# Summing gathered rows feature-major: the gathered rows become the stationary operand, and the copy and transpose of each window's sums go

## The chip, the cores and the metric

The kernel runs on one core of a Trainium2 chip. The metric is the device time of one execution in microseconds (us). TensorE is called PE here (its weight loads are a row of their own, PEld), VectorE DVE, ScalarE ACT, GpSimd POOL, and SyncE SP.

## What is computed

Two graph networks in a row over 2,500 nodes of 256 features and 82,500 edges, sorted by the node that receives them. All is float32. The part that the change touches is the first network, which has two layers:

```
edge_index = stack([src, dst])
for l in range(2):                       # RelGraphConv with a basis
    W = einsum('rb,bio->rio', coeff[l], basis[l])      # 8 relations
    all_h = einsum('ni,rio->rno', h, W)
    msg = all_h[etype, src] * norm
    h = segment_sum(msg, dst, 2500) + bias[l]          # relu after the first
x = layernorm(x + h)
```

The second network (an input product, three layers of `relu(mean of neighbours @ W_agg + h @ W_self + b)`, an output product, a layer norm of x plus the result) runs after it, in the "mean layers" below.

## The kernel before

**Tiles and windows.** The edges are cut into T = 645 tiles of 128. For each tile POOL issues an indirect DMA (`rows_of`, L250) that gathers the 128 source rows (1 KB each) into one of NG = 16 slots of `G`. DVE builds a selector `S` of 128 x 128 (L455, one of NSL = 8 slots): the row of an edge holds its weight in column 16 * relation + (destination minus the window's first node). Three tiles (TA = 3) make a window, of which a layer has NA = 215. PE sums the three tiles of a window in a PSUM bank (L662): `S` is stationary, the gathered rows move, and the sum is node-major, 128 selector columns on the partitions and 256 features along the bank.

**Turning the sums.** The later product wants them with the features on the partitions. So ACT copies each window's sum to `Zs` (L560), PE transposes its two halves into bank 4 or 5 (`pe_turn`, L650), and DVE adds them at the window's place in `ZA` (`dve_add`, L444), where ten windows overlap. After ten windows (30 tiles, a large window) PE multiplies `ZA` by the relations' weights, sixteen products spread over eight tiles (`pe_apply`, L615), adds what is carried over (L620), and ACT copies the product out (L519).

**Beside it.** Between the tiles, the kernel counts the edges between each two nodes for the second network: DVE builds two one-hot tables per tile (L378, L379), PE multiplies them (L593) and carries a window's overlap on (L598), ACT casts the counts (L505, L508), SP stores them. DVE also mixes the weights of the relations.

**The order.** Each engine's program is unrolled, and tile t comes in the same place on all of them. Waits are on semaphores that only count up:

- POOL gathers tile n once tile n - 16 has been summed (`s_sum`).
- DVE builds the selector of tile t + 5 at step t, once tile t - 3 has been summed. At each step with t % 3 = 1 it then adds window (t - 4) // 3, after that window's transposes (`s_turn`).
- ACT copies a window after its third tile (`s_sum`), and reports with `s_zs`.
- PE waits for a tile's rows (`s_land`) and selector (`s_sel`). At each step with t % 3 = 1 it transposes the window that ended two tiles earlier. Written for window k: tile 3k+2 ends it, PE goes on with tiles 3k+3 and 3k+4, and then waits for the copy of window k (`s_zs`) before anything behind it can start. `pe_turn` also waits for the addition of window k - 2 (`s_za`).

Both layers go this way one after the other, 1,290 tiles in all. Then come the mean layers (`pe_mean_layers`), with no gathers, in which PE multiplies counts by node rows (L828). L319 loads a register with a window's place, L494 clears `ZA`.

Of the kernel before, what the change touches and what calls it, by code (L numbers as in the profile page):

```python
# [94 lines left out]
def program(nc, x, ramp, ramp_col, srcT, dstT, etT, wT, large, small, basis, coeff, bias, W_in, b_in, W_agg, W_self,  # L95
# [11 lines left out]
    with ExitStack() as ctx:  # L107
# [3 lines left out]
        def sem(name):  # L111
            return ctx.enter_context(nc.semaphore(name))
# [59 lines left out]

        with ExitStack() as inner:
            RY = inner.enter_context(nc.sbuf_tensor("RY", [128, 20480], F32))
        (Mr, Nr, Aw, Aw8, E2, G, S, Zs, W2, ZA, Ew, Pg, hw, h1w, xw, xT) = lay(
            RY, ((NSL, 128), BF16), ((NSL, NB), BF16), ((4, NB), BF16), ((4, NB), U8), ((2, 128), BF16), ((NG, 256), F32),
            ((NSL, 128), F32), ((2, 256), F32), ((2, 2048), F32), ((2, 16 * ZC), F32), ((2, 128), F32), ((2, 256), F32),
            ((2, 256), F32), ((2, 256), F32), ((2, 256), F32), ((2, 256), F32))
        ZA = ZA.rearrange("p s (q c) -> p s q c", c=ZC)
        diag = [v[:, k, h * 128:(h + 1) * 128] for v in (xw, xT) for k in range(2) for h in range(2)]  # L180
# [5 lines left out]
        x1b = sb("x1b", [128, 4, 256], F32)  # L186
        assert EARLY * 512 + NR * CH <= 8512

        bank = [ctx.enter_context(nc.psum_tensor(f"bank{i}", [128, 512], F32)) for i in range(8)]


        s_src, s_dst, s_et, s_wgt, s_base, s_bas0, s_bas1, s_wts = (
# [5 lines left out]
        s_land = [sem(f"s_land{i}") for i in range(NG)]  # L198
        s_sel, s_sum = sem("s_sel"), sem("s_sum")

        s_zs, s_turn, s_za = sem("s_zs"), sem("s_turn"), sem("s_za")

        s_clear, s_carry1, s_prod, s_pg = sem("s_clear"), sem("s_carry1"), sem("s_prod"), sem("s_pg")
        s_hw, s_h1w, s_h1 = sem("s_hw"), sem("s_h1w"), sem("s_h1")
# [228 lines left out]
        def dve_add(e, l, w):  # L433

            g, wi = divmod(w, SW)
            wg = l * NA + w
            r = row_base(e, off[0:1, w:w + 1], 127)
            o = ZA[:, g % 2, :, bass.ds(r, 16)]
            if wi == 0:
                e.wait_ge(s_clear, 4 * (l * NW + g + 1))  # L440
            else:
                e.wait_ge(s_za, wg)
            e.wait_ge(s_turn, wg + 1)
            e.tensor_tensor(o, o, bank[4 + wg % 2][:, 0:256].rearrange("p (q c) -> p q c", c=16), ALU.add).then_inc(s_za, 1)  # L444

        def dve_layer(e, l):
            for t in range(T + (TAIL if l == 0 else 2)):
# [97 lines left out]
        def act_layer(e, l):  # L545
            for t in range(T + (TAIL if l == 0 else 2)):
                n = l * T + t
                if t == 0:
                    if l == 0:
                        e.wait_ge(s_zero, 1)  # L550
                    for k in range(4):
                        act_clear(e, l, 0, k)
                if t % TW in (24, 25, 26, 27) and t // TW + 1 < NW and t < T:
                    act_clear(e, l, t // TW + 1, t % TW - 24)
                if t % TA == TA - 1 and t < T:
                    wg = l * NA + t // TA
                    if wg > 1:
                        e.wait_ge(s_turn, wg - 1)
                    e.wait_ge(s_sum, n + 1)
                    e.copy(Zs[:, wg % 2, :], bank[2 + wg % 2][:, 0:256]).then_inc(s_zs, 1)  # L560
                for g, k in STEPS[l].get(t, []):
                    act_post(e, l, g, k)
                if l == 0 and t < 8 * WPE:
                    act_weight(e, t)
                if t < T:
                    for a in COUNTS.get(n, []):
                        act_counts(e, a)
                    if n in A_LOADS:
                        j = A_LOADS.index(n)
                        if j == 0:  # L570
                            e.wait_ge(s_ad, 16 * NA)
                            e.wait_ge(s_chore, NCH)
                            e.wait_ge(s_w1p, 8 * WPE)
                            e.wait_ge(s_prod, NW)
                        e.dma_start(A_sb[0:PB, j, :], Ad[j * PB:(j + 1) * PB, 0:N]).then_inc(s_A, 16)
# [63 lines left out]
                                      xT[:, s, c * 128:(c + 1) * 128], start=(c == 0), stop=(c == 1))  # L639
                mm.then_inc(s_win, 1)  # L640

        def pe_turn(e, l, w):
            wg = l * NA + w
            if wg > 1:
                e.wait_ge(s_za, wg - 1)
            else:
                e.wait_ge(s_idn, 1)
            e.wait_ge(s_zs, wg + 1)
            for c in range(2):
                mm = e.transpose(bank[4 + wg % 2][:, c * 128:(c + 1) * 128], Zs[:, wg % 2, c * 128:(c + 1) * 128], idn[:, :])  # L650
            mm.then_inc(s_turn, 1)

        def pe_layer(e, l):
            for t in range(T + (TAIL if l == 0 else 2)):
                n = l * T + t
                if t < T:
                    i, wg, k = t % TA, l * NA + t // TA, edge_rows(t)
                    if i == 0 and wg > 1:
                        e.wait_ge(s_zs, wg - 1)
                    e.wait_ge(s_sel, n + 1)  # L660
                    e.wait_ge(s_land[n % NG], 16 * (n // NG + 1))
                    e.matmul(bank[2 + wg % 2][:, 0:256], S[0:k, n % NSL, :], G[0:k, n % NG, :], start=(i == 0),  # L662
                             stop=(i == TA - 1)).then_inc(s_sum, 1)
                for g, k in STEPS[l].get(t, []):
                    if k < 8:
                        pe_apply(e, l, g, k)
                    elif l == 1:
                        pe_post(e, g, k)
                if t >= 4 and t % TA == 1 and t - 2 < T:
                    pe_turn(e, l, (t - 4) // TA)  # L670
                if l == 0 and t < 8 * WPE:
                    pe_weight(e, t)
                if t < T:
                    for a in COUNTS.get(n, []):
                        pe_counts(e, a)
# [137 lines left out]
        def pe_aggregate(e, l, c, j):  # L813
            n, i = (l * NC + c) * JB + j, l * NC + c
            bs = (2 * (i % 2), 2 * (i % 2) + 1)
            if j == 0:
                if i == 0:
                    e.wait_ge(s_pg, 2 * NW)
                    e.wait_ge(s_put, 2 * (NW - 1))
                elif i == 1:  # L820
                    e.wait_ge(s_zs, 2 * NA)
                else:
                    e.wait_ge(s_mean, 2 * (i - 1))
            e.wait_ge(*converted(n))
            e.wait_ge(s_lo, l * JB + j + 1)
            for mo in range(2):
                for q in range(2):
                    mm = e.matmul(bank[bs[mo]][:, 0:CH], hs[0:PB, j, q, mo * 128:(mo + 1) * 128], Ar[0:PB, n % NR, :],  # L828
                                  start=(j == 0 and q == 0), stop=(j == JB - 1 and q == 1))
            mm.then_inc(s_agg, 1)  # L830
# [43 lines left out]
        def sp_load_x1(e, j):  # L874
            if j == 0:
                e.wait_ge(s_x1d, 16 * NW)
                e.wait_ge(s_x1t, NW)
            if j >= 4:
                e.wait_ge(s_y, j - 3)
            e.dma_start(x1b[0:PB, j % 4, :], X1[j * PB:(j + 1) * PB, :]).then_inc(s_x1b[j % 4], 16)  # L880
# [81 lines left out]

        def act_mean_layers(e):
            last = NW - 1
            e.wait_ge(s_turn, 2 * NA)
            e.wait_ge(s_ad, 16 * NA)
            e.wait_ge(s_A, 16 * JB)
            for n in range(NR):
# [26 lines left out]

        def dve_mean_layers(e):
            last = NW - 1
            e.wait_ge(s_turn, 2 * NA)
            e.wait_ge(s_ad, 16 * NA)
            dve_carry1(e, 1, last)  # L1000
            for j in range(4):
# [404 lines left out]
```

## Time and profile before

| | |
|---|---|
| runs shown | 2393.61, 2394.03, 2397.88 us |
| median | 2394.03 us |
| the profiled execution's own time | 2401.69 us |
| its span, first to last instruction | 2399.9 us |
| mean granted PE clock in it | 0.889 of full speed |
| busy: PE, PEld, DVE, ACT, POOL | 75%, 56%, 50%, 26%, 52% of the span |

The busy share of PE counts recorded matmuls, whose ends the profiler models. The idle time of an engine stands behind the group of instructions that it precedes, with what ended it; "issue" is time for which the profile shows no wait, "remote" a release that it could not put down to an instruction. The gathers run to about 1,975 us, and the rest is the mean layers.

### The profile page before, as it was taken

Reading aid. Unit: us, or ns where it says so; the run is one execution under the profiler, and the core shown is the slowest. Engines: PE = TensorE matmul, PEld = TensorE weight load, DVE = VectorE, ACT = ScalarE, POOL = GpSimd, SP = SyncE. Lnnn points to the kernel's source line nnn. Section 1 sums busy time; section 2 is a strip of 40 time slices with the busy share of each in tenths; the row PEclk is TensorE's granted clock in tenths of the full one; section 3 lists DMA queues with packets and bytes.
Section 4 is the critical chain, followed back from the end, with each engine's and each line's share of the span. In section 5 each row is a group of like instructions: output and inputs, shape, how many; then the busy total and the mean of one; then the engine's idle time right before and its main releaser. Section 6 shows DMA issues by size and latency. Waiting matters only on the chain.

```text
span 2399.9 us, 29813 instructions
## 1 busy us (share of the span) xinstructions
PE 1803.5 (75%) x7695; PEld 1342.2 (56%) x7695; DVE 1197.4 (50%) x3965; ACT 625.7 (26%) x1520; POOL 1255.5 (52%) x1294
## 2 busy tenths in 40 slices
PE   4667677677677676757677777776666679999997
PEld 2455455455455454535455555555555567777776
DVE  5747654544445445335555555553268743232355
ACT  1112222222222222212222322222111124633332
POOL 5766666666666666366666666666666630000000
PEclk9879888988889899879989888899888789999998
DMA  6333333333333333233333333334533320000011
GB/s 209 93 89 97 99 98 98 100 97 98 99 99 97 99 99 99 59 92 101 102 100 98 105 99 100 103 101 122 169 102 96 98 61 11 1 1 1 1 35 44
DMA packets 118622, 208.19 MB, mean 87 GB/s; under 512 B 53828, under 2 KB 74196, under 8 KB 118456
## 3 DMA queue, kind: packets, MB, share of 16 engines
q0 software_dynamic: 62016, 169.04, 24.8%
q1 hardware_dynamic: 48848, 26.08, 3.8%
q10 hardware_dynamic: 7592, 11.13, 1.4%
q8 instruction: 71, 1.16, 0.2%
q14 instruction: 95, 0.78, 0.1%
HBM read 189.01 MB, written 17.13 MB: 86 GB/s over the span
## 4 chain that ended last, share of the span: by engine, by line
PE 50%; another core or an unknown queue 17%; issue 14%; DVE 13%; ACT 3%; DVEq 2%; DMA 1%; ACTq 0%; POOL 0%
PE bank L662 15%; PE bank L828 11%; PE bank L615 8%; DVE RY L455 4%; PE bank L650 4%; DVE RY L444 2%; PE bank L593 2%; PE bank L845 2%; PE bank L773 2%; DVE RY L379 1%; DVE RY L378 1%; DMA RX<-in_basis 1%; ACT RY L560 1%; DVE rdeg L390 1%
## 5 line engine op out<-in xcount | busy, mean ns | idle before, releaser
L662 PE MATMUL bank<-RY 128*128 128x256 f32 x2580 | 864.3, 432 | 11.6 <-issue 4.6
L250 POOL DMA_INDIRECT RY<-H,si x645 | 619.4, 960 | 367.0 <-issue 152.4
L250 POOL DMA_INDIRECT RY<-in_x,si x645 | 635.8, 986 | 333.1 <-issue 147.5
L444 DVE TENSOR_TENSOR RY<-RY,bank 128x256 f32 x430 | 180.8, 420 | 900.7 <-remote 694.8
L662 PEld LDWEIGHTS bank<-RY 128*128 128x128 f32 x2580 | 487.1, 220 | 109.4 <-issue 42.0
L650 PE MATMUL bank<-idn,RY 128*128 128x128 f32 x860 | 193.4, 311 | 394.7 <-issue 245.9
L455 DVE TENSOR_SCALAR RY<-iot,c,wgt 128x128 f32<-128x128 f32 x1290 | 461.8, 370 | 1.5 <-issue 1.5
L560 ACT COPY RY<-bank 128x256 f32<-128x256 f32 x430 | 161.1, 375 | 973.2 <-PE bank L662 519.8
L650 PEld LDWEIGHTS bank<-idn,RY 128*128 128x128 f32 x860 | 116.5, 158 | 503.4 <-issue 451.0
L828 PE MATMUL bank<-Ar,hs 125*128 125x500 f32 x1200 | 305.8, 405 | 0.0
L828 PEld LDWEIGHTS bank<-Ar,hs 125*128 125x128 f32 x1200 | 225.7, 188 | 51.7 <-issue 9.2
L593 PE MATMUL bank<-RY 128*128 128x320 bf16 x645 | 214.1, 333 | 16.2 <-DVE RY L379 8.4
L615 PE MATMUL bank<-RX,RY 128*128 128x256 f32 x704 | 202.8, 417 | 29.3 <-issue 25.3
L615 PE MATMUL bank<-RY 128*128 128x256 f32 x704 | 198.7, 410 | 18.6 <-DVE RY L444 12.7
L379 DVE TENSOR_SCALAR RY<-iotN,bcol 128x320 bf16<-128x320 f16 x645 | 196.0, 304 | 0.0
L615 PEld LDWEIGHTS bank<-RX,RY 128*128 128x128 f32 x704 | 146.8, 211 | 59.7 <-issue 31.5
L378 DVE TENSOR_SCALAR RY<-iotN,c 128x128 bf16<-128x128 f16 x645 | 178.9, 277 | 0.0
L615 PEld LDWEIGHTS bank<-RY 128*128 128x128 f32 x704 | 143.8, 206 | 47.3 <-DVE RY L444 16.1
L505 ACT CAST RY<-bank 128x320 bf16<-128x320 f32 x215 | 92.2, 429 | 249.3 <-remote 190.5
L740 ACT CAST Ar<-RX 125x500 fp32r<-125x500 uint8 x200 | 119.2, 609 | 99.2 <-PE bank L828 99.1
L494 ACT COPY RY<-zero 128x576 f32<-128x576 f32 x176 | 113.3, 680 | 0.0
L593 PEld LDWEIGHTS bank<-RY 128*128 128x128 bf16 x645 | 68.8, 107 | 69.0 <-issue 32.5
(106 smaller groups left out, 1163.2 us busy)
## 6 DMA issues: line engine op xcount, KB each, us to landing
RY<-in_x,si POOLq DMA_INDIRECT x645
RY<-H,si POOLq DMA_INDIRECT x645
Ad<-RY SPq DMA_DIRECT2D x215, 40.0 KB
RX<-Ad ACTq DMA_DIRECT2D x20, 305.2 KB
RX<-in_basis ACTq DMA_DIRECT2D x2, 2048.0 KB, 34.3
H<-RY SPq DMA_DIRECT2D x22, 128.0 KB
RY<-in_x SPq DMA_DIRECT2D x22, 128.0 KB
X<-RY SPq DMA_DIRECT2D x22, 128.0 KB
```

Source lines behind the costliest of these rows:

```text
L250: e.indirect_dma_start(G[0:k, n % NG, :], None, table, bass.IndirectOffsetOnAxis(ap=si[0:k, t:t + 1], axis=0)).then_inc(s_land[n % NG], 16)
L378: e.tensor_scalar(Mr[:, u % NSL, :], iotN[:, 0:128], c1[:, u:u + 1], None, ALU.is_equal)
L379: e.tensor_scalar(Nr[:, u % NSL, :], iotN[:, :], bcol[:, u:u + 1], None, ALU.is_equal).then_inc(s_hot, 1)
L444: e.tensor_tensor(o, o, bank[4 + wg % 2][:, 0:256].rearrange("p (q c) -> p q c", c=16), ALU.add).then_inc(s_za, 1)
L455: e.tensor_scalar(S[:, v % NSL, :], iot[:, :], c2[:, u:u + 1], wgt[:, u:u + 1], ALU.is_equal, ALU.mult).then_inc(s_sel, 1)
L560: e.copy(Zs[:, wg % 2, :], bank[2 + wg % 2][:, 0:256]).then_inc(s_zs, 1)
L593: e.matmul(b[:, 0:NB], Mr[0:k, a % NSL, :], Nr[0:k, a % NSL, :], start=(i == 0), stop=(w == 0 and i == TA - 1)).then_inc(s_cnt, 1)
L615: mm = e.matmul(bank[0][:, 0:256], ZA[:, s, q, 0:128], W[:, c, r * 256:(r + 1) * 256], start=(q == 0), stop=(g == 0 and q == 15))
L650: mm = e.transpose(bank[4 + wg % 2][:, c * 128:(c + 1) * 128], Zs[:, wg % 2, c * 128:(c + 1) * 128], idn[:, :])
L662: e.matmul(bank[2 + wg % 2][:, 0:256], S[0:k, n % NSL, :], G[0:k, n % NG, :], start=(i == 0), stop=(i == TA - 1)).then_inc(s_sum, 1)
L740: e.copy(o, i_).then_inc(s_arA, 1)
L828: mm = e.matmul(bank[bs[mo]][:, 0:CH], hs[0:PB, j, q, mo * 128:(mo + 1) * 128], Ar[0:PB, n % NR, :], start=(j == 0 and q == 0), stop=(j == ...
```

## The change

PE sums the tiles the other way round: half of the gathered rows (128 features) is stationary, and the selector moves. A tile takes two matmuls of 128 columns, one for each half of the features, in place of one of 256. The sum stands feature-major in PSUM at once. The two halves go to two banks (2 and 4, or 3 and 5 for the other window of a pair), which are now declared as one tensor of two banks (`pair`), so that DVE adds both with one instruction, straight from the sums. The ACT copy, `Zs`, the transposes, and the semaphores `s_zs` and `s_turn` go. DVE's addition stays at its step and now waits for `s_sum`. The first tile of window k waits for the addition of window k - 2.

```diff
-        (Mr, Nr, Aw, Aw8, E2, G, S, Zs, W2, ZA, Ew, Pg, hw, h1w, xw, xT) = lay(
+        (Mr, Nr, Aw, Aw8, E2, G, S, W2, ZA, Ew, Pg, hw, h1w, xw, xT) = lay(
...
-        bank = [ctx.enter_context(nc.psum_tensor(f"bank{i}", [128, 512], F32)) for i in range(8)]
+        pair = [ctx.enter_context(nc.psum_tensor(f"pair{i}", [128, 2, 512], F32)) for i in range(2)]
+        bank = [None if i in (2, 3, 4, 5) else ctx.enter_context(nc.psum_tensor(f"bank{i}", [128, 512], F32)) for i in range(8)]
+        for i in range(4):
+            bank[2 + i] = pair[i % 2][:, i // 2, :]
...
# dve_add
-            o = ZA[:, g % 2, :, bass.ds(r, 16)]
+            o = ZA[:, g % 2, :, bass.ds(r, 16)].rearrange("p (a b) c -> p a b c", a=2)
...
-            e.wait_ge(s_turn, wg + 1)
-            e.tensor_tensor(o, o, bank[4 + wg % 2][:, 0:256].rearrange("p (q c) -> p q c", c=16), ALU.add).then_inc(s_za, 1)
+            e.wait_ge(s_sum, l * T + min(T, TA * w + TA))
+            e.tensor_tensor(o, o, pair[wg % 2][:, :, 0:128].rearrange("p a (b c) -> p a b c", c=16), ALU.add).then_inc(s_za, 1)
...
# act_layer
-                if t % TA == TA - 1 and t < T:
-                    wg = l * NA + t // TA
-                    if wg > 1:
-                        e.wait_ge(s_turn, wg - 1)
-                    e.wait_ge(s_sum, n + 1)
-                    e.copy(Zs[:, wg % 2, :], bank[2 + wg % 2][:, 0:256]).then_inc(s_zs, 1)
...
-        def pe_turn(e, l, w):
-            wg = l * NA + w
-            if wg > 1:
+        def pe_sums_of(e, l, t):
+
+            n, i, wg, k = l * T + t, t % TA, l * NA + t // TA, edge_rows(t)
+            if i == 0 and wg > 1:
                 e.wait_ge(s_za, wg - 1)
-            else:
-                e.wait_ge(s_idn, 1)
-            e.wait_ge(s_zs, wg + 1)
+            e.wait_ge(s_sel, n + 1)
+            e.wait_ge(s_land[n % NG], 16 * (n // NG + 1))
             for c in range(2):
-                mm = e.transpose(bank[4 + wg % 2][:, c * 128:(c + 1) * 128], Zs[:, wg % 2, c * 128:(c + 1) * 128], idn[:, :])
-            mm.then_inc(s_turn, 1)
+                mm = e.matmul(bank[2 + 2 * c + wg % 2][:, 0:128], G[0:k, n % NG, c * 128:(c + 1) * 128], S[0:k, n % NSL, :],
+                              start=(i == 0), stop=(i == TA - 1))
+            mm.then_inc(s_sum, 1)
...
# pe_layer
-                    i, wg, k = t % TA, l * NA + t // TA, edge_rows(t)
-                    if i == 0 and wg > 1:
-                        e.wait_ge(s_zs, wg - 1)
-                    e.wait_ge(s_sel, n + 1)
-                    e.wait_ge(s_land[n % NG], 16 * (n // NG + 1))
-                    e.matmul(bank[2 + wg % 2][:, 0:256], S[0:k, n % NSL, :], G[0:k, n % NG, :], start=(i == 0),
-                             stop=(i == TA - 1)).then_inc(s_sum, 1)
+                    pe_sums_of(e, l, t)
...
-                if t >= 4 and t % TA == 1 and t - 2 < T:
-                    pe_turn(e, l, (t - 4) // TA)
```

At the ends of the layers, the waits for `s_zs`, `s_turn` and `s_x1t` become waits for `s_za`, `s_sum` and `s_win`.

The order on PE before, from tile 180 of the first layer, which begins window 60 (L662 sums a tile, L650 is a transpose, L593 and L598 are the counts, L615 a product of `ZA`):

```order
L662 MATMUL bank2<-RY 128x256 [waits s_land4,s_sel,s_zs]
L593 MATMUL bank6<-RY 128x320 [waits s_hot,s_aw8]
L662 MATMUL bank2<-RY 128x256 [waits s_land5,s_sel]
L650 MATMUL bank5<-idn,RY 128x128 [waits s_zs,s_za]
L650 MATMUL bank5<-idn,RY 128x128
L662 MATMUL bank2<-RY 128x256 [waits s_land6,s_sel]
L593 MATMUL bank6<-RY 128x320 [waits s_hot]
L662 MATMUL bank3<-RY 128x256 [waits s_land7,s_sel,s_zs]
```

The same stretch of the changed kernel (L648 sums half a tile, L591 is a count):

```order
L648 MATMUL pair0<-RY 128x128 [waits s_land4,s_sel,s_za]
L648 MATMUL pair0<-RY 128x128
L591 MATMUL bank6<-RY 128x320 [waits s_hot,s_aw8]
L648 MATMUL pair0<-RY 128x128 [waits s_land5,s_sel]
L648 MATMUL pair0<-RY 128x128
L648 MATMUL pair0<-RY 128x128 [waits s_land6,s_sel]
L648 MATMUL pair0<-RY 128x128
L591 MATMUL bank6<-RY 128x320 [waits s_hot]
L648 MATMUL pair1<-RY 128x128 [waits s_land7,s_sel,s_za]
```

Between the second and the third tile stood two transposes of the window before, with a wait for its copy. Now nothing stands there, and a window's first tile waits for an addition in place of a copy.

On DVE before, at step 181, which adds window 59:

```order
L455 TENSOR_SCALAR RY<-iot,c2,wgt 128x128 [waits s_sum]
L319 TENSOR_LOAD off
L319 ISA x2
L444 ISA [waits s_turn,s_za]
L444 TENSOR_TENSOR RY<-RY,bank5 128x16x16
L455 TENSOR_SCALAR RY<-iot,c2,wgt 128x128 [waits s_sum]
```

And of the changed kernel:

```order
L459 TENSOR_SCALAR RY<-iot,c2,wgt 128x128 [waits s_sum]
L323 TENSOR_LOAD off
L323 ISA x2
L448 ISA [waits s_sum,s_za]
L448 TENSOR_TENSOR RY<-RY,pair1 128x16x16
L459 TENSOR_SCALAR RY<-iot,c2,wgt 128x128 [waits s_sum]
```

The addition stands where it stood; only what it waits for is another semaphore.

## Rows read from the trace of the kernel before

**Rows 1.** The page: span, busy time by engine, and POOL in 40 slices.

```profile
span 2399.9 us, 29813 instructions
...
PE 1803.5 (75%) x7695; PEld 1342.2 (56%) x7695; DVE 1197.4 (50%) x3965; ACT 625.7 (26%) x1520; POOL 1255.5 (52%) x1294
...
POOL 5766666666666666366666666666666630000000
```

**Rows 2.** Stretches of 100 us: busy us (instructions) by engine, PEclk, DMA share, GB/s.

```profile
100.00:200.00 100.00, 64.01 (x253) 47.09 (x251) 51.69 (x155) 16.31 (x41) 67.52 (x69) 0.78 0.33 95
500.00:600.00 100.00, 75.01 (x329) 54.35 (x328) 48.71 (x203) 25.46 (x67) 65.57 (x68) 0.87 0.35 99
1700.00:1800.00 100.00, 70.37 (x288) 56.15 (x287) 52.32 (x111) 15.68 (x40) 64.56 (x69) 0.83 0.43 127
```

**Rows 3.** The page's costliest groups: busy, mean ns, idle before them and releaser.

```profile
L662 PE MATMUL bank<-RY 128*128 128x256 f32 x2580 | 864.3, 432 | 11.6 <-issue 4.6
L250 POOL DMA_INDIRECT RY<-H,si x645 | 619.4, 960 | 367.0 <-issue 152.4
L250 POOL DMA_INDIRECT RY<-in_x,si x645 | 635.8, 986 | 333.1 <-issue 147.5
L444 DVE TENSOR_TENSOR RY<-RY,bank 128x256 f32 x430 | 180.8, 420 | 900.7 <-remote 694.8
L662 PEld LDWEIGHTS bank<-RY 128*128 128x128 f32 x2580 | 487.1, 220 | 109.4 <-issue 42.0
L650 PE MATMUL bank<-idn,RY 128*128 128x128 f32 x860 | 193.4, 311 | 394.7 <-issue 245.9
L560 ACT COPY RY<-bank 128x256 f32<-128x256 f32 x430 | 161.1, 375 | 973.2 <-PE bank L662 519.8
```

**Rows 4.** POOL's waits: us in total, times, longest.

```profile
POOL RY L250 <- PE bank L662: 210.9, 222, 9.8
POOL RY L250 <- remote: 151.8, 107, 2.5
POOL RY L250 <- DMA H<-RY: 33.0, 1, 33.0
```

**Rows 5.** Timeline from 621.9 us: start, duration, instruction, idle before it.

```profile
621.90 0.38 PE L650 MATMUL bank<-idn,RY 128*128 128x128 f32 x2
...
622.11 0.60 PE L662 MATMUL bank<-RY 128*128 128x256 f32 x2
...
622.55 0.30 PE L593 MATMUL bank<-RY 128*128 128x320 bf16 x1
...
624.25 0.59 PE L662 MATMUL bank<-RY 128*128 128x256 f32 x2
625.20 0.94 POOL L250 DMA_INDIRECT RY<-in_x,si  x1 [0.30 <-issue]
626.06 0.37 ACT L560 COPY RY<-bank 128x256 f32<-128x256 f32 x1 [4.43 <-PE bank L662]
...
626.45 0.95 POOL L250 DMA_INDIRECT RY<-in_x,si  x1 [0.30 <-issue]
...
626.58 0.41 PE L650 MATMUL bank<-idn,RY 128*128 128x128 f32 x2 [1.73 <-issue]
```

**Rows 6.** Timeline of PE from 650 us.

```profile
650.71 0.60 PE L662 MATMUL bank<-RY 128*128 128x256 f32 x2
...
651.85 0.59 PE L662 MATMUL bank<-RY 128*128 128x256 f32 x2
659.09 0.66 PE L650 MATMUL bank<-idn,RY 128*128 128x128 f32 x2 [6.65 <-issue]
```

**Rows 7.** Timeline of ACT from 650 us.

```profile
658.57 0.37 ACT L560 COPY RY<-bank 128x256 f32<-128x256 f32 x1 [2.21 <-remote]
```

**Rows 8.** Timeline of PE from 1,230 us: eight float32 passes of 128 columns.

```profile
1236.25 1.05 PE L638 MATMUL bank<-RY,wts 128*128 128x128 f32 x8
1237.14 0.30 PE L593 MATMUL bank<-RY 128*128 128x320 bf16 x1
```

More of the change, by code:

```diff
@@ L174, in program @@
             RY = inner.enter_context(nc.sbuf_tensor("RY", [128, 20480], F32))
-        (Mr, Nr, Aw, Aw8, E2, G, S, Zs, W2, ZA, Ew, Pg, hw, h1w, xw, xT) = lay(
+        (Mr, Nr, Aw, Aw8, E2, G, S, W2, ZA, Ew, Pg, hw, h1w, xw, xT) = lay(
             RY, ((NSL, 128), BF16), ((NSL, NB), BF16), ((4, NB), BF16), ((4, NB), U8), ((2, 128), BF16), ((NG, 256), F32),
-            ((NSL, 128), F32), ((2, 256), F32), ((2, 2048), F32), ((2, 16 * ZC), F32), ((2, 128), F32), ((2, 256), F32),
+            ((NSL, 128), F32), ((2, 2048), F32), ((2, 16 * ZC), F32), ((2, 128), F32), ((2, 256), F32),
             ((2, 256), F32), ((2, 256), F32), ((2, 256), F32), ((2, 256), F32))
@@ L199, in program @@
         s_sel, s_sum = sem("s_sel"), sem("s_sum")
-        s_zs, s_turn, s_za = sem("s_zs"), sem("s_turn"), sem("s_za")
+        s_za = sem("s_za")
         s_clear, s_carry1, s_prod, s_pg = sem("s_clear"), sem("s_carry1"), sem("s_prod"), sem("s_pg")
@@ L820, in pe_aggregate @@
                 elif i == 1:
-                    e.wait_ge(s_zs, 2 * NA)
+                    e.wait_ge(s_za, 2 * NA)
                 else:
@@ L876, in sp_load_x1 @@
                 e.wait_ge(s_x1d, 16 * NW)
-                e.wait_ge(s_x1t, NW)
+                e.wait_ge(s_win, NW)
             if j >= 4:
@@ L964, in act_mean_layers @@
             last = NW - 1
-            e.wait_ge(s_turn, 2 * NA)
+            e.wait_ge(s_sum, 2 * T)
             e.wait_ge(s_ad, 16 * NA)
@@ L997, in dve_mean_layers @@
             last = NW - 1
-            e.wait_ge(s_turn, 2 * NA)
+            e.wait_ge(s_sum, 2 * T)
             e.wait_ge(s_ad, 16 * NA)
```

## The prediction

> **What bounds the kernel now.** I read the page first [rows 1]. No engine is busy all the time: PE 75% of the span and POOL 52%, and POOL's slices are at 6 tenths, evenly, until the gathers end at about 1,975 us. The mean layers behind them have no gathers and no window sums, so the change can only act before. There are 430 windows of three tiles.
>
> The stretches [rows 2] say how this part keeps time. POOL issues 68 or 69 gathers in 100 us, that is 1.45 to 1.47 us for a tile and 4.35 to 4.41 us for a window. It does so with the counts (500 to 600 us, PE busy 75.0) and without them (100 to 200 and 1,700 to 1,800 us, PE busy 64.0 and 70.4). Work comes and goes on PE and the pace stays: the amount of PE's work is not the bound.
>
> POOL itself could go faster. Two gathers that nothing holds up start 1.25 us apart [rows 5], 0.95 us of work and 0.30 us of its own issue. Its idle time is 367.0 + 333.1 = 700.1 us [rows 3]. Of this 1290 x 0.30 = 387 us is its own issue, and 33.0 us the wait for the first layer's rows [rows 4]. The other 280 us is waiting for a slot, that is for PE to report tile n - 16 as summed ("PE bank L662" and "remote").
>
> Why is PE late, if it has time? The timeline [rows 5] shows it. PE transposes at 621.90 us, sums the next tile at 622.11 us and two more by 624.85 us, and stands still for 1.73 us until the next transposes at 626.58 us. These wait for ACT's copy, which starts at 626.06 us, although the matmuls of the window's last tile end at 622.71 us by the record and ACT has been idle for 4.43 us. So the report of that sum reached ACT about 3.35 us late. Thirty microseconds on it is worse: sum over at 651.31 us [rows 6], copy at 658.57 us [rows 7], 7.26 us later, and PE idle for 6.65 us. I don't know what delays these reports. That they are late is what sets the pace: transposes of window k - 1, last sum of window k, report, copy, transposes of window k. Each window makes this round trip by itself. It costs 0.21 (transposes) + 0.44 (sum) + 0.37 (copy) + the delay, and some 0.15 us of signalling, so 1.2 us + the delay. The mean of 4.4 us leaves 3.2 us for the delay and for PE's other work before the transposes. The idle time ahead of the copies, 973.2 us, and ahead of the transposes, 394.7 us [rows 3], is this trip seen from two engines.
>
> **The change, part by part.**
>
> *Sums.* 1290 tiles change from two recorded passes of 256 columns to four of 128 (a float32 matmul has two). Before, a tile takes 622.55 - 622.11 = 0.44 us [rows 5]. Eight float32 passes of 128 columns with weights of their own, back to back, take 1237.14 - 1236.25 = 0.89 us [rows 8], 0.111 us each, so four take 0.44 us. A window stays at 1.33 us. The weight load's own row has a mean of 220 ns [rows 3]. If it were not hidden, a tile would take 0.88 us; that is the upper bound, and 0.44 us the lower one. I take 0.44 us, because rows 8 are the same shape and type. The Trainium skill, "Perfetto Trace Analysis", Matmuls, says that larger matmuls are more efficient than smaller ones when possible. By it PE's work would grow; it gives no figure, and between these two rows the trace does not bear it out.
>
> *Transposes.* 430 pairs of 0.21 us go from PE, 90 us. They lie beside waiting, and are worth nothing by length alone. With them goes the wait in which PE stood.
>
> *Copies.* 430 copies of 375 ns go from ACT (161 us busy [rows 3]). ACT bounds nothing at 26%, so only their place in the trip counts.
>
> *Addition.* DVE's instruction has as many elements, from two banks. The nearest row is the present one, 420 ns; two instructions' worth, 840 ns, is the upper bound. DVE has 900.7 us of idle time ahead of it [rows 3], which hides 181 us more. I take no change. It stands at the same step of DVE's order. Behind it are the selectors, but those of five tiles ahead are made by then; it now waits for a sum instead of a transpose made two tiles later, so it comes free earlier.
>
> *New wait.* The first tile of window k waits for the addition of window k - 2, hence for the report of tile 3k - 4, and three tiles lie between. At POOL's own pace four tiles take 5.0 us. Of these 0.44 us is the sum, 0.42 us the addition and some 0.1 us signalling, so that delays up to 4.0 us cost nothing. Before, at that pace, the limit was 3.75 - 1.2 = 2.6 us. More than this margin counts that two windows are in the trip together: a batch of late reports lets six tiles through, where it now lets through three, and the 16 slots then absorb what is left.
>
> *The ends of the layers* save one copy and one pair of transposes each, about 1 us. I leave it out.
>
> *The sum.* With no wait for slots, POOL would bound: 2401.7 (the profiled execution) - 280 = 2122 us. One of the two delays that I looked at (7.26 us) is far beyond 4.0 us, so some stops of PE stay, and the slots do not cover all of them. I take two thirds of the 280 us as gone, 187 us: 2215 us. The ends that I keep are all of it and a third. The median of the runs shown is 7.7 us below the profiled execution, which gives **2207 us**.
>
> **The rivals.**
>
> *R1, POOL bounds.* The delays stay as they are, the slots cover them, and all 280 us go: 2122 - 7.7 = **2114 us**. For it: PE has idle time in every stretch [rows 2]. Against it: delays of 7 us.
>
> *R2, the reports come later still.* POOL's pauses go, and if the reports are delayed by the traffic of the gathers, each stop comes back at the addition's wait. A third of the 280 us is gained: 2401.7 - 93 - 7.7 = **2301 us**. For it: PE lay idle for 6.65 us while a report was still out [rows 6, 7], so the delay is not PE's own queue. Against it: I can't see a link to the gathers in these rows.
>
> *R3, slower.* The place is PE's completion of the sums. If the gap between recorded end and report is real work of PE that the record hides, PE has no spare time, and more passes cost their time in full. A window's sums and transposes are now 6 + 2 passes (2580 and 860 over 430 windows [rows 3]), and become 12. Four more at 0.111 us [rows 8] are 191 us, which gives 2394 + 191 = **2585 us**; at the weight load's 0.22 us they would be 378 us, 2772 us. It decides once PE's true time for a window is above 4.4 us. For it: nothing else in the rows explains the late reports. Against it: the pace is the same with and without the counts' passes [rows 2], and 6.65 us of idle PE is longer than any work queued before it. The Trainium skill, "Perfetto Trace Analysis", Tensor Engine Instruction, says that the profiler only estimates when a matmul ends. By that the gap may be hidden work, and R3 would be the case; the rows bear it out only in that the reports are late.
>
> *R4, no change.* What holds POOL is not this trip, or the addition's wait takes its place one for one: **2394 us**.
>
> **How the numbers follow.** A measurement of this kernel can tell about 0.2%, 5 us, from no change. Forecast (2130 to 2290 us) 0.50, R1 0.13, R2 (2290 to 2389 us) 0.17, R4 0.07, R3 0.13. So faster 0.80, same 0.07, slower 0.13. The range goes from just below R1, 2105 us, to R4, 2390 us. Beyond it lie R3, most of R4 and a little of R1, about 0.2. The forecast alone would have 2130 to 2290 us.
>
> **What would show it.** Right: more than 72 gathers in 100 us (the forecast has 1290 x 1.25 + 93 us of waiting, 1.32 us each, so 75 or 76); POOL's waits for L648 under 150 us; no ACT row for a copy; four passes of a tile in about 0.44 us; gathers over by about 1,790 us; the mean layers as long as before, some 425 us. R1: 80 gathers in 100 us. R2: PE idle ahead of the first tile of a window, released by DVE's addition, often for 3 us and more. R3: PE's idle time gone and under 68 gathers in 100 us, or passes of L648 0.2 us apart at the full clock. My argument fails if the pace stays while the copies are gone.

## The result, and the profile after

The change makes no gain: 2401.97 us median (2396.86 to 2405.13, 20 runs) against 2397.06 us (2392.14 to 2399.77, 20 runs) for the kernel before, beside it on the same chip. The ratio is 1.0023, 95% interval 1.0016 to 1.0029. I had predicted 2,207 us.

The page of the profiled execution after: span, busy time by engine, POOL in 40 slices.

```profile
span 2400.1 us, 31965 instructions
...
PE 1782.9 (74%) x9415; PEld 1484.7 (62%) x9415; DVE 1219.4 (51%) x3965; ACT 481.8 (20%) x1090; POOL 1246.4 (52%) x1294
...
POOL 5766666666666666466666666666666640000000
```

Against [rows 1] ACT has lost its 430 copies (1520 instructions became 1090), PE has 1,720 records more (2,580 more passes for sums, 860 fewer for transposes), and POOL looks the same in every slice.

The same stretches as in [rows 2]: busy us (instructions) of PE, PEld, DVE, ACT and POOL, PEclk, DMA share, GB/s.

```profile
100.00:200.00 100.00, 59.05 (x321) 51.14 (x321) 51.84 (x151) 7.87 (x19) 66.45 (x68) 0.78 0.33 93
500.00:600.00 100.00, 71.02 (x403) 59.09 (x402) 49.60 (x197) 17.89 (x44) 63.80 (x68) 0.87 0.35 98
1700.00:1800.00 100.00, 69.13 (x397) 61.58 (x395) 53.28 (x109) 7.99 (x18) 64.81 (x69) 0.84 0.43 129
```

Still 68 or 69 gathers in 100 us. Where did the waits go? The costliest groups (busy, mean ns, idle before them and releaser), to be read against [rows 3]:

```profile
L648 PE MATMUL pair<-RY 128*128 128x128 f32 x5160 | 907.9, 320 | 487.0 <-issue 251.5
L648 PEld LDWEIGHTS pair<-RY 128*128 128x128 f32 x5160 | 819.8, 228 | 625.5 <-issue 320.1
L254 POOL DMA_INDIRECT RY<-in_x,si x645 | 631.8, 980 | 341.6 <-issue 152.9
L254 POOL DMA_INDIRECT RY<-H,si x645 | 614.3, 952 | 370.8 <-issue 148.0
L459 DVE TENSOR_SCALAR RY<-iot,c,wgt 128x128 f32<-128x128 f32 x1290 | 450.3, 356 | 562.4 <-PE pair L648 374.0
L448 DVE TENSOR_TENSOR RY<-RY,pair 128x256 f32 x430 | 180.5, 420 | 314.3 <-remote 166.9
```

The addition is the same size (420 ns). PE had 394.7 us of idle time ahead of its transposes and 11.6 us ahead of its sums; now 487.0 us stand ahead of the sums. The list of waits (us in total, times, longest) says what for, as far as the profile shows a release:

```profile
PEld pair L648 <- issue: 320.1, 222, 6.5
POOL RY L254 <- issue: 300.8, 981, 1.1
PEld pair L648 <- DVE RY L448: 259.7, 129, 10.8
PE pair L648 <- issue: 251.5, 159, 6.1
POOL RY L254 <- PE pair L648: 223.9, 201, 5.7
PE pair L648 <- DVE RY L448: 217.7, 110, 10.2
...
POOL RY L254 <- remote: 157.2, 106, 3.3
```

PE now waits for DVE's addition, up to 10.2 us (and 251.5 us more with no release on record), and POOL waits 223.9 + 157.2 = 381 us for slots, where it waited 363 us [rows 4]. The timeline shows one stop (start, duration, instruction, idle before it):

```profile
620.15 0.61 PE L648 MATMUL pair<-RY 128*128 128x128 f32 x4
...
620.60 0.30 PE L591 MATMUL bank<-RY 128*128 128x320 bf16 x1
...
622.04 0.61 PE L648 MATMUL pair<-RY 128*128 128x128 f32 x4
...
622.73 0.30 PE L591 MATMUL bank<-RY 128*128 128x320 bf16 x1
623.47 0.35 DVE L459 TENSOR_SCALAR RY<-iot,c,wgt 128x128 f32<-128x128 f32 x1 [3.38 <-PE pair L648]
623.63 0.43 ACT L509 CAST RY<-bank 128x320 bf16<-128x320 f32 x1 [9.45 <-remote]
623.71 0.94 POOL L254 DMA_INDIRECT RY<-in_x,si  x1 [1.91 <-PE pair L648]
...
624.29 0.42 DVE L448 TENSOR_TENSOR RY<-RY,pair 128x256 f32 x1 [0.47 <-issue]
...
624.77 0.83 PE L648 MATMUL pair<-RY 128*128 128x128 f32 x4 [1.74 <-DVE RY L448]
```

DVE, ACT and POOL all start within 0.24 us of each other, after 3.38, 9.45 and 1.91 us of idling. The trace has a mark for a semaphore's update: three marks of the sums' reports and two of the counts' stand between 623.45 and 623.70 us. So a handful of PE's reports arrived together, and everyone who waited for one of them woke.

I followed this through the trace, from the recorded end of each sum to the next mark of its semaphore. Some marks are missing (there are 1,184 for 1,290 sums), so single delays are rough. Once the gathers are over, PE's marks come 0.01 us after the ends. In the gather part the median in each 100 us is 1.0 to 1.9 us from 100 to 1,700 us, and a tenth come over 3.4 us late. Only PE's are late: of DVE's reports on its selectors more marks are missing (753 stand for 1,290), but nine tenths of those in the gather part stand 0.01 us after an end, where by the same measure PE's stand 1.1 us after one in the median.

### The profile page after: what moved, and what is told of

It reads as the page before. It is cut to its first block, busy times and chain, and to the rows that moved or that the text cites. A ratio compares the mean times of both kernels' runs of the same rounds, so it can differ in the third digit from the quotient of the medians.

```text
span 2400.1 us, 31965 instructions
## 1 busy us (share of the span) xinstructions
PE 1782.9 (74%) x9415; PEld 1484.7 (62%) x9415; DVE 1219.4 (51%) x3965; ACT 481.8 (20%) x1090; POOL 1246.4 (52%) x1294
## 4 chain that ended last, share of the span: by engine, by line
PE 63%; issue 13%; another core or an unknown queue 11%; DVE 9%; DMA 1%; DVEq 1%; ACT 1%; ACTq 0%; POOL 0%; SPq 0%; POOLq 0%
PE pair L648 28%; PE bank L613 12%; PE bank L819 6%; PE pair L819 5%; PE bank L591 3%; DVE RY L459 3%; DVE RY L448 2%; PE pair L836 2%; PE bank L764 2%; PE bank L636 1%; DMA RX<-in_basis 1%; PE bank L596 1%; DVEq L323 1%; DVE RX L359 1%
## 5 line engine op out<-in xcount | busy, mean ns | idle before, releaser
L648 PE MATMUL pair<-RY 128*128 128x128 f32 x5160 | 907.9, 320 | 487.0 <-issue 251.5
L648 PEld LDWEIGHTS pair<-RY 128*128 128x128 f32 x5160 | 819.8, 228 | 625.5 <-issue 320.1
L254 POOL DMA_INDIRECT RY<-in_x,si x645 | 631.8, 980 | 341.6 <-issue 152.9
L254 POOL DMA_INDIRECT RY<-H,si x645 | 614.3, 952 | 370.8 <-issue 148.0
L448 DVE TENSOR_TENSOR RY<-RY,pair 128x256 f32 x430 | 180.5, 420 | 314.3 <-remote 166.9
L591 PE MATMUL bank<-RY 128*128 128x320 bf16 x645 | 216.5, 336 | 7.7 <-issue 3.9
L613 PE MATMUL bank<-RY 128*128 128x256 f32 x704 | 201.3, 413 | 7.3 <-DVE RY L448 5.6
L819 PE MATMUL bank<-Ar,hs 125*128 125x500 f32 x640 | 166.0, 406 | 0.0
L613 PEld LDWEIGHTS bank<-RY 128*128 128x128 f32 x704 | 133.8, 210 | 21.8 <-DVE RY L448 5.8
L819 PE MATMUL pair<-Ar,hs 125*128 125x500 f32 x560 | 142.1, 403 | 0.0
L819 PEld LDWEIGHTS bank<-Ar,hs 125*128 125x128 f32 x640 | 120.3, 188 | 27.6 <-issue 5.0
L819 PEld LDWEIGHTS pair<-Ar,hs 125*128 125x128 f32 x560 | 105.4, 188 | 24.1 <-issue 4.1
L523 ACT COPY RY<-bank 128x256 f32<-128x256 f32 x44 | 16.4, 372 | 431.3 <-remote 340.4
```

Source lines behind the costliest of these rows:

```text
L254: e.indirect_dma_start(G[0:k, n % NG, :], None, table, bass.IndirectOffsetOnAxis(ap=si[0:k, t:t + 1], axis=0)).then_inc(s_land[n % NG], 16)
L448: e.tensor_tensor(o, o, pair[wg % 2][:, :, 0:128].rearrange("p a (b c) -> p a b c", c=16), ALU.add).then_inc(s_za, 1)
L591: e.matmul(b[:, 0:NB], Mr[0:k, a % NSL, :], Nr[0:k, a % NSL, :], start=(i == 0), stop=(w == 0 and i == TA - 1)).then_inc(s_cnt, 1)
L613: mm = e.matmul(bank[0][:, 0:256], ZA[:, s, q, 0:128], W[:, c, r * 256:(r + 1) * 256], start=(q == 0), stop=(g == 0 and q == 15))
L648: mm = e.matmul(bank[2 + 2 * c + wg % 2][:, 0:128], G[0:k, n % NG, c * 128:(c + 1) * 128], S[0:k, n % NSL, :], start=(i == 0), stop=(i == ...
```

## The experiments

The runs fell on several chips, and these are of two kinds. Each time is to be read beside the kernel before on the same chip. On two of the five chips the kernel before took 2,107 and 2,109 us (**prompt** chips below), on three, and on the one of the result, 2,371 to 2,398 us (**late** chips). Where no number of executions is given, it is one.

### Four cuts through the whole

Half the bytes of each gather (the sums take this half of the features twice; the cuts of code below show the lines that matter):

```diff
-G[0:k, n % NG, :], None, table, ...            # 1 KB for a row
+G[0:k, n % NG, 0:128], None, half, ...         # table as (2N, 128), 512 B
```

> The change with half the bytes of every gather: 128 columns of a row in place of 256 (the sums use this half twice, so the output is another one). Theory T (the traffic of the gathers holds back PE's reports): with half the bytes a report comes in half the delay, the pace rises from 68 to over 73 gathers in 100 us, below 2,250 us. Theory P (PE's own time for its work, hidden by the record, sets the pace): no change, 2,390 to 2,410 us. Theory D (POOL's issue, not bytes): no change either.

One pass in place of two for each sum, `G` and `S` read as the upper halves of their float32:

```diff
+            G16 = G[0:k, n % NG, :].bitcast(BF16).rearrange("p (c h) -> p c h", h=2)[:, :, 1]   # S16 alike
...
```

> The change with the sums taken from the upper 16 bits of the rows and selectors, as bfloat16: two passes in a tile in place of four (the sums lose accuracy). Theory P: PE's time for a window falls by 6 of its 12 passes, so the pace rises at once to what POOL can do, under 2,200 us. Theory T: PE's work is beside the point, within 1% of 2,400 us. Theory D: the same as T.

Every sum twice:

```diff
-            for c in range(2):
+            for j in range(4):
+                c = j % 2
...
```

> The change with every sum taken twice (eight passes for a tile, 0.89 us in place of 0.44; the sums are twice as large). Theory P: 12 more passes in a window at 0.11 us or more, so at least 430 x 1.33 = 572 us longer, 2,970 us or more. Theory T and D: PE has room in a window of 4.4 us, 2,400 to 2,500 us, and the longer time only in the stretches where PE was nearly full.

No gathers after the first sixteen:

```diff
-            for n in range(FIRST, 2 * T):
+            for n in ():
...
# pe_sums_of
-            e.wait_ge(s_land[n % NG], 16 * (n // NG + 1))
+            e.wait_ge(s_land[n % NG], 16)
```

> The change without the gathers after the first 16 (PE sums these 16 tiles again and again; POOL is idle and H1 is not read). All other work and waits stay. Theory P: the pace stays, 2,350 to 2,400 us. Theory T: reports come at once, and the gather part (1,930 us) shrinks to what PE and DVE need, under 1,500 us, in all under 1,950 us. Theory D gives the same time as T, but T alone says that sums are reported in under 0.3 us here.

Measured: half bytes 2093.34, one pass 2105.85, twice 2118.27, no gathers 1632.94 us, and the kernel before 2107.22 us. This was a prompt chip, which none of the expectations had foreseen, so these times don't decide between their theories. With PE's work halved or doubled the time stays within 0.6% of the kernel before, and without the gathers it falls by 474 us: on this chip POOL's 1.25 us a gather is the bound. Twice the sums, stretch 500 to 600 us (columns as above):

```profile
500.00:600.00 100.00, 100.00 (x790) 94.65 (x790) 59.31 (x230) 20.00 (x49) 75.92 (x80) 1.00 0.41 115
```

PE is busy all the time and POOL still issues 80 gathers. In all four traces no 100 us of the gather part has a median or a 90th percentile of the report's delay above 0.01 us, and in the three that gather the gathers are faster than in the result. So gathers do not make reports late on every chip.

### The change and the kernel before again, POOL set free, fewer slots

> The change itself, word for word, timed against the kernel before on a chip on which the kernel before took 2,107 us in place of 2,397. On such a chip PE's reports were never late (0.01 us in four kernels). Theory T2 (late reports are a condition of the chip and set the pace only where they occur; elsewhere POOL's 1.25 us does): the change takes 2,100 to 2,115 us, within 0.5% of before, 79 gathers in 100 us. Theory L (the change is slower by its own work on DVE or PE): the difference of 5 us of the other chip stays or grows. On a chip of the slow kind: 2,402 against 2,397 us again.

> The kernel before, word for word, for its trace. T2: where it takes 2,107 us, its copies L560 start within 0.3 us of the end of the sum, POOL's waits for PE are under 60 us, and PE's stops ahead of the transposes are short. If its trace shows late reports at 2,107 us too, T2 falls.

POOL free: the gathers go round 15 slots that nobody reads, PE sums the rows in slot 0 again and again, and a tile's sum still waits for its gather's landing.

```diff
-                if n >= NG:
-                    e.wait_ge(s_sum, n - NG + 1)
+                e.wait_ge(s_land[slot(n)], 16 * (n_before(n)))   # landed before
...
```

> The change with POOL set free: PE sums slot 0 for every tile, the gathers go round the other 15 slots and wait for nothing but their slot's last landing; a tile's sum still waits until its gather has landed (the sums are of other rows). Theory T2, chip with prompt reports: POOL was waiting for little, 0 to 20 us gained, 1.25 to 1.27 us for each gather. Chip with late reports: gathers at 1.25 us, and the sums stay behind them by more than 16 tiles if the traffic holds the reports back (over 2,450 us), or follow them (2,120 us) if the 16 slots were the trouble.

Twelve slots:

```diff
-NG = 16
+NG = 12
...
-FIRST = 16
+FIRST = 12
```

> The change with 12 slots for gathered tiles in place of 16. Theory T2, chip with prompt reports: PE is seldom 12 tiles behind, 2,105 to 2,130 us. Chip with late reports: the pauses of POOL come earlier but the pace is set by the reports, within 1% of 2,402 us; if instead the slots' slack decides, over 2,450 us.

This was a late chip. The change took 2405.21 us (7 executions) against 2397.92 (10; ratio 1.0031, 1.0016 to 1.0046), the kernel before once more 2397.47, twelve slots 2400.01, and POOL set free **3290.91 us**. Its page shows PE and POOL in 40 slices of 82 us, and the granted clock between them:

```profile
PE   2100011101189999930001111011899987899998
...
POOL 7777777777500000067777777776000000000000
PEclk8555555555599999965555555555899998999999
```

While POOL gathers, PE does almost nothing; when POOL has finished a layer, PE catches up at full speed. By stretches:

```profile
100.00:200.00 100.00, 15.86 (x36) 8.63 (x35) 7.50 (x16) 1.17 (x3) 75.94 (x80) 0.52 0.36 104
500.00:600.00 100.00, 17.11 (x42) 11.71 (x43) 7.26 (x14) 0.00 (x0) 76.21 (x73) 0.52 0.33 95
...
1100.00:1200.00 100.00, 100.00 (x739) 91.74 (x738) 86.38 (x364) 32.10 (x78) 0.00 (x0) 1.00 0.07 18
```

And a piece of the timeline inside the first layer:

```profile
322.71 2.93 PE L655 MATMUL pair<-RY 128*128 128x128 f32 x12 [30.67 <-issue]
...
333.25 0.34 DVE L464 TENSOR_SCALAR RY<-iot,c,wgt 128x128 f32<-128x128 f32 x1 [9.02 <-remote]
...
344.45 0.34 DVE L464 TENSOR_SCALAR RY<-iot,c,wgt 128x128 f32<-128x128 f32 x1 [10.06 <-remote]
...
355.84 0.42 DVE L453 TENSOR_TENSOR RY<-RY,pair 128x256 f32 x1 [11.04 <-issue]
```

PE sums three tiles by 325.64 us. DVE, idle, gets one report 7.6 us later, the next 11.2 us after that, and the third, which lets it add, another 11 us later. The rows themselves landed as always: by the DMA packets, the last of a gather ended 2.4 us after its issue in the median, here, in the change and on the prompt chip. In the two stretches in which PE catches up there are no gathers, and the reports come 0.01 us after the sums' ends. So on this late chip it is the gather stream that holds back PE's reports, not PE's queue and not rows that come late. That goes with the second outcome named before the run (over 2,450 us). In the change POOL's wait for slots keeps it from coming to this: it stops POOL, and reports get through. The kernel without gathers never ran on a late chip.

### Is it the depth of the buffers, the bytes, or PE's work?

Four windows in flight: the six matmuls of a window are issued together at its third tile, so both halves fit one bank, and there are 14 selectors.

```diff
# pe_sums_of
-            if i == 0 and wg > 1:
-                e.wait_ge(s_za, wg - 1)
+            if t % TA < TA - 1:
+                return
+            if wg >= 4:
+                e.wait_ge(s_za, wg - 3)
...
```

> The change with more room for PE to run ahead of its own reports: the six matmuls of a window are issued together at its third tile, so that a window needs one PSUM bank and four windows are in flight in place of two, and 14 selectors in place of 8. Theory T2, chip with late reports: POOL's pauses are what lets the reports through, and each pause now frees up to 12 tiles in place of 6, so half of the 280 us of pauses goes, 2,250 to 2,300 us. Theory B (the balance between gathers and PE is in time, not in tiles: PE needs its share of the time without gathers however deep the buffers are): within 1% of 2,402 us. On a chip with prompt reports: 2,100 to 2,115 us.

The 14 selectors alone, made up to eleven tiles ahead:

```diff
-AHEAD = 6
+NSS = 14        # slots of S
+AHEAD = 12
...
```

> The change with 14 selectors in place of 8, nothing else. T2, late reports: two windows in flight still limit PE to six tiles, so no more than 1% from 2,402 us. B: the same. If it alone gains over 3%, it was DVE's selectors that made PE stop, and not the addition. Prompt reports: 2,100 to 2,115 us.

Two of the first four again, for a late chip:

> Half the bytes of every gather (128 columns of a row in place of 256, the sums use this half twice) once more, for a chip with late reports. If the bytes hold the reports back: over 73 gathers in 100 us, under 2,250 us. If it is the number of rows or POOL's own work on a gather: within 2% of 2,402 us. Prompt reports: 2,093 us again.

> Every sum taken twice once more (eight passes for a tile), for a chip with late reports. Theory T2 and B with reports as the scarce thing: PE has room, under 2,450 us. Theory B with PE's working time as the scarce thing: each microsecond of passes needs its own stretch without gathers, 1290 x 0.44 = 568 us more, 2,900 us or above. Prompt reports: 2,118 us again.

A late chip, the kernel before at 2371.18 us. Four windows 2378.66, selectors 2376.51, half bytes 2371.22, sums twice 2423.90 us. My theory that a stop frees as many tiles as PE may run ahead is wrong: with room for twelve POOL still gets 68 to 70 gathers in 100 us. Half the bytes bring nothing, so the amount of data is not the load. Doubling the sums, where PE needs 91 us of 100, costs about 2%:

```profile
500.00:600.00 100.00, 90.59 (x672) 82.28 (x671) 50.23 (x196) 17.14 (x42) 62.79 (x67) 0.98 0.35 98
```

### Data or descriptors, even spacing or full stops, number of reports

Gathers of 64 bytes for a row from the 17th tile on:

```diff
+            c = 256 if n < NG else 16
+            part = table if n < NG else table.rearrange("n (a b) -> (n a) b", b=16)
...
```

> The change with 64 bytes gathered for a row in place of 1,024 (from the 17th tile on; the sums are of other numbers), with as many rows, descriptors and instructions. If the data hold PE's reports back, they come at once now and the gathers run at 1.25 us: under 2,150 us. If descriptors or POOL's work do it: within 1.5% of the change, 67 to 69 gathers in 100 us. On a chip with prompt reports 2,090 to 2,110 us and nothing is told apart.

A memset of 128 columns on POOL after each gather, for which the next gather waits:

```diff
                 rows_of(e, n, x if n < T else H1)
...
+                e.memset(pause, 0.0).then_inc(s_pause, 1)
```

> The change with a short memset on POOL between two gathers, so that they start further apart (1.35 to 1.6 us) and evenly. Theory S (the pace is a time share: PE needs some 0.2 us without gather work for each tile, whenever it comes): if the spacing is up to 1.5 us, the pauses for slots shrink by as much and the time stays within 1.5% of the change. Theory F (reports come only when the gathers have stopped altogether): the pauses stay and the spacing adds to them, at least 1290 x 0.1 = 130 us more. Prompt reports: 1290 x spacing + 490 us.

The four windows again, with one report for each (the cut is against the four windows):

```diff
-                    if c == 1:
-                        mm.then_inc(s_sum, 1)
+            mm.then_inc(s_sum, 1)
...
```

> The change with four windows, 14 selectors and one report of PE for a window in place of three. If the number of PE's reports is what the path can't carry: 3% or more faster than the kernel before on this chip. If not: within 1% of it, as the same kernel with three reports was (2,379 against 2,371 us).

> The change without the gathers after the first 16, once more, for a chip with late reports. If the gathers alone hold the reports back: 1,633 us as on the chip with prompt reports (within 1.5%), and no late report. If the chip has slow reports by itself: over 1,700 us.

These fell on a prompt chip, the kernel before at 2108.86 us: tiny rows 2101.10, spaced 2220.12, one report 2104.19, no gathers 1628.65 us. They tell little of the late chips. Even 64 bytes for a row leave POOL at its 1.25 us, so that time does not depend on the bytes. The memset stretched the 1.25 us to 1.34 us and cost 111 us against the kernel before, close to 1274 x 0.09 = 115.

The last two:

> The change itself, timed again. On a chip with prompt reports (before at 2,107 to 2,109 us): POOL's 1.25 us for a gather is the bound of both kernels, so the change takes 2,104 to 2,112 us, within 0.3% of before. If the copies and transposes did cost something there, it is 0.5% faster or more. On a chip with late reports: 0.2 to 0.3% slower than before again.

> The change with a short memset on POOL after each gather, which stretched the 1.25 us between gathers to 1.34 us on the chip with prompt reports (2,220 us). On a chip with late reports: theory S (time share: what POOL leaves idle counts, whenever it does) has the pauses shrink by what the memsets take, within 1.5% of the change; theory F (reports pass only when the gathers have stopped altogether) has the pauses stay, 2,400 + 116 = 2,516 us or so. Prompt reports: 2,220 us again.

A late chip. The change took 2378.93 us (10 executions) against 2374.70 (13; ratio 1.0017, 1.0004 to 1.0029); with the memsets it took 2381.24 us. What cost 111 us on the prompt chip costs 2.3 us here. POOL's waits in the change on this chip:

```profile
POOL RY L254 <- PE pair L648: 177.8, 184, 5.6
POOL RY L254 <- remote: 167.6, 119, 4.0
```

and with the memsets:

```profile
POOL RY L254 <- PE pair L651: 102.9, 122, 5.8
POOL RY L254 <- remote: 77.0, 80, 2.4
```

345 us of waiting for slots became 180 us, and within the layers the gathers still start 1.48 us apart in the mean, as without the memsets. The expectation for a time share holds, the one for full stops (2,516 us) does not.

### What follows

| kernel | time, us | before on the same chip | kind | POOL's wait for slots, us |
|---|---|---|---|---|
| the change | 2405.2, 2378.9 | 2397.9, 2374.7 | late | 381, 345 |
| the kernel before | 2397.5 | 2397.9 | late | 369 |
| 12 slots | 2400.0 | 2397.9 | late | 386 |
| 4 windows with 14 selectors | 2378.7 | 2371.2 | late | 342 |
| 14 selectors alone | 2376.5 | 2371.2 | late | 342 |
| half bytes | 2371.2 | 2371.2 | late | 341 |
| sums twice | 2423.9 | 2371.2 | late | 430 |
| spaced | 2381.2 | 2374.7 | late | 180 |
| POOL free | 3290.9 | 2397.9 | late | none |
| half, tiny bytes | 2093.3, 2101.1 | 2107.2, 2108.9 | prompt | 157, 84 |
| one pass; twice | 2105.9; 2118.3 | 2107.2 | prompt | 80; 127 |
| one report | 2104.2 | 2108.9 | prompt | 35 |
| spaced | 2220.1 | 2108.9 | prompt | 40 |
| no gathers | 1632.9, 1628.7 | 2107.2, 2108.9 | prompt | |

(The last column adds POOL's waits for PE and "remote". Each has 0.3 us of POOL's own issue in it; half bytes on the prompt chip has 491 of them in its 157 us, so that hardly any waiting is left there.) On a late chip gathers and PE's reports share something. With POOL free the gathers come 1.25 to 1.42 us apart, by stretches of 100 us, and in the first layer PE sums 55 tiles between 100 us and the last gather at 881 us, one in 14 us; at 1.48 us in the mean, stops included, PE keeps up. The slots find that point by themselves, whatever the trip around them looks like, and for that reason neither buffers nor spacing nor the removed copies and transposes move it. That the gathers hold back the reports is shown by POOL set free. That a balance in time sets the pace is borne out by the spacing and the deeper buffers, one execution each; what lies between 1.42 and 1.48 us was not tried. What is shared is not known: not the data (half bytes), not PE's passes (5,160 more of them cost 9 ns each: 2423.9 - 2371.2 = 52.7 us over the kernel before, less the 4.2 us by which the change was slower on another late chip, is 48.5 us). Descriptors and the number of reports were to be told apart by tiny rows and one report, but both ran on a prompt chip only, and this stays open.

## Why the prediction was wrong, point by point

**What bounds the kernel.** Right: the amount of PE's work doesn't, and POOL could go at 1.25 us. The sum without any wait for slots, 2122 - 8 = 2114 us, is within 0.4% of what prompt chips show for the kernel before (2107.22, 2108.86). Wrong: the step "that they are late is what sets the pace", by the round trip transposes, sum, report, copy. The lateness was taken as given, a fixed delay that the trip adds up. On a late chip it is an answer to the gathers. I wrote that I don't know what delays the reports and went on to forecast what happens if the delay stays the same; it doesn't stay the same when POOL speeds up.

**Sums.** Right. Four passes take 0.45 us (620.15 to 620.60 us in the timeline), where 0.44 us was forecast. The Trainium skill, "Perfetto Trace Analysis", Matmuls, prefers larger matmuls; in this row the step from 256 to 128 columns costs 0.01 us a tile. **Addition** 420 ns, right. **Copies and transposes**: gone, worth nothing, as their length alone was said to be.

**New wait.** Its margin, delays up to 4.0 us, fitted the delays before, of which by the marks 8% are longer. But PE stops at it for 218 us in all, up to 10.2 us. In the stop that the timeline shows, the burst that lets DVE add is the same that lets POOL go on; that most stops are of this kind was not counted.

**The sum.** The failed step is "I take two thirds of the 280 us as gone", which rests on "That they are late is what sets the pace". None went. The sum that gave 280 us gives 299.5 us for the change: 341.6 + 370.8 us idle, less 387 us of issue and 25.9 us for the first layer's rows. In the list of waits 363 us became 381. In place of the trip, the runs show gathers and reports in balance: three ways around the slots (two windows in flight, four windows, 12 slots) give the same pace, and POOL without its stops leaves PE one tile in 14 us.

**The rivals.** R4, "what holds POOL is not this trip", 2,394 us, was the case and had 0.07. R2 had the mechanism, "if the reports are delayed by the traffic of the gathers, each stop comes back at the addition's wait", but let a third of the 280 us be gained; nothing was. Its sign was there before: PE idle for 6.65 us while a report was out [rows 6], and, in the trace of before, PE's marks 0.01 us after the ends wherever there were no gathers. R1's 2114 us is the prompt chip's time, though not by this change. R3 is refuted: 5,160 added passes cost some 48 us on a late chip and 11 us on a prompt one, not 0.111 us each. The Trainium skill, "Perfetto Trace Analysis", Tensor Engine Instruction, says that a matmul's end is estimated; the delay of 7.6 us after three tiles on an otherwise idle PE is no hidden work of that kind, because in the same trace the same passes are reported in 0.01 us once a layer's gathers are over.

**What would show it.** The signs did their work: gathers in 100 us (over 72 for right, found 68), POOL's waits for L648 (under 150 us, found 224), the last gather (by 1,790 us, found 1,958), all with the copies gone, as my sentence on what makes the argument fail has it. Of R2's sign, PE stopped by the addition often for 3 us and more, there are 110 stops of 2.0 us in the mean.

**The small loss.** The three measurements on late chips agree, 0.2 to 0.3%, 4 to 7 us. At the 9 ns above, 1,720 more passes would be 16 us, an estimate; what the copies and transposes that are gone give back was not measured, so the cause of the loss is not shown. What the change does on a prompt chip was not timed as it stands. Its neighbours there (one pass, one report) are 1.4 and 4.7 us below the kernel before, one run each.

## What to carry to other kernels

If a report is late while its engine idles, ask first where in the program it is late and where it isn't, and what else runs there. The trace of before answers it, and that would have been a reason to move chance from the forecast to R2 and R4. A ring of slots that seems to be too slow may be the regulator of something shared; a kernel that sets it free can show this in one run (here 3,291 us). And time a kernel beside its reference on more than one chip before a bound is taken for the kernel's own.

## What the hardware showed that I had not expected

- Two kinds of chips: 2,107 and 2,109 us on two, 2,371 to 2,398 us on the others, for the same program. The difference, 262 to 291 us, lies nearly all in the gather part: the last gather is issued at 1,958 us in the change (late) and at 1,681 us in the sums twice (prompt), and 442 and 436 us follow it.
- On the late chip POOL itself slows when it never waits: in the free kernel 80 gathers in the stretch from 100 us, 73 in the one from 500 us, without any wait for slots. On the prompt chip it gets 80 in the stretch from 500 us.
- On late chips the profile also lacks most marks of the gathers' landings: about 4,500 of 20,640 in the traces of before and after, 2,323 with POOL free, 20,536 with the sums twice on the prompt chip. The 4-byte writes themselves are all recorded as DMA packets, so it is the marks that are lost. The Trainium skill, "NOTIFIC — the notification-queue block", section Interfaces, says that a full internal queue of the trace records can stall the engines that write them. Whether that is the shared thing, and the late chips' delay a part of being profiled, no run here shows; it is a rival that stays open.
- PE's granted clock was 0.52, the level of 1.2 GHz, in the stretches in which PE was busy for 16 and 17 us of 100, and 1.00 (2.4 GHz) in the one in which it caught up.
